# A macaron transformer layer on one core: the first quad's operands are spread by TensorE and its maxima added on chip, the opening runs in halves, and the steps of every batch are placed anew

## The chip, the cores and the metric

The kernel runs on one core of one Trainium2 chip. The metric is the device time of one execution in microseconds; the times given are medians of several runs. An engine has its own queue of instructions and runs it in order: TensorE (PE in the rows, PEld for its weight loads), VectorE (DVE), ScalarE (ACT), GpSimd (POOL) and SyncE (SP), which here issues most transfers. They wait for each other by semaphores alone.

## The reference

Eight batches of 512 tokens with 128 channels pass through half a feed-forward, attention, and half a feed-forward.

```python
x = x + 0.5 * ffn(layernorm(x), W1, b1, W2, b2)      # ternary W1, W2; ReLU; 128 -> 512 -> 128
x = x + attn(layernorm(x), Wq, bq, ...)              # 16 heads of 8 channels, RoPE on q and k
x = x + 0.5 * ffn(layernorm(x), W1, b1, W2, b2)
...
scores = einsum('bhnd,bhmd->bhnm', q, k) / sqrt(8)   # 512 x 512 per head and batch
attn = softmax(scores); out = einsum('bhnm,bhmd->bhnd', attn, v)
```

All of it is float32. The first feed-forward is called ffn1 here, the second ffn2.

## The kernel before

**Scores.** Heads go in pairs, eight pairs a batch, two pairs to a quad; the two heads of a pair lie in rows 0 to 63 and 64 to 127 of the array. q and k are each split into a high and a low part, and the four products of parts of eight channels fill 32 of a head's 64 rows. Rows 62 and 63 are for the maxima: k's hold -1 and q's the high and low part of each query's maximum, so that the second product comes out as score less maximum. The operands in that layout are `q_stack` and `k_stack`, with two slots for batches in turn. They are filled through memory: the parts go to `q_scratch` and `k_scratch` (`part_to_scratch`, L403), and from there as rows to the stack (`rows_to_stack`, L409). Rows that no transfer fills are set to zero by ScalarE (`zeros`, L796), and k's -1 by a transfer (`minus_between`).

**Steps.** A batch has 32 steps. In each, TensorE makes one score pair for the maxima (`m`, L541; VectorE reduces it, L906) and one transposed score pair (`e`, L560; ScalarE takes its exponential, L788). A burst `pv` (L577) multiplies four heads' probabilities with v. Score pairs lie in three units of PSUM in turn; one is free when its maximum or exponential has been taken. At the end of a quad VectorE splits the maxima, TensorE transposes them (`max_T`), ScalarE copies them and SP writes them into the stack.

**Order.** The lists FIRST (batch 0), STEADY (1 to 3) and LATER (4 to 7) give the order in words, the same for every engine: beside `e`, `m` and `pv` stand the side work of other batches (`ffn1_up0@3` is the first quarter of ffn1's hidden layer of batch 3), in one bank of PSUM, `side`. Each feed-forward is a transposition `T`, four `up` of two products (high and low part of x in float16) and four `down`. ffn1 runs four batches ahead, the projections two.

**Opening.** PROLOGUE lists what stands ahead of the steps: ffn1 of batch 0, T and up of batch 1, attention's transposition and first projections (`k_first`, `q_first`, each with a cosine and a sine part, rotated on VectorE, L983 to L989), v, down of batch 1 and T and up of batch 2. Then come eight maxima (OPEN_MAX), with down of batch 2 between the first four. Products with `ones_f` (`fill`, L652) write nothing that is used. The first quad's maxima go in as two half quads of four (`first_max_T`, L602, L760).

**End.** The last batch's attention output and ffn2 run in halves on all engines.

## Time and profile before

| | us |
|---|---|
| median of 3 runs | 520.1 (518.65 to 523.45) |
| the profiled execution, its time | 519.27 |
| its span | 517.5 |
| TensorE busy | 488.3 |
| VectorE busy | 409.2 |
| ScalarE busy | 347.5 |
| GpSimd busy | 203.5 |
| first score pair of TensorE at | 43.31 |
| its first transposed score pair at | 54.67 |
| last exponential ends at | 497.6 |

Busy time is a union of an engine's instructions; waits and issue are not in it. The ends of matmuls are modelled, so that a full TensorE is not at its peak. The granted clock is TensorE's, as a share of 2.4 GHz. A name after an arrow in brackets is what ended an engine's idle time.

### The profile page before, as it was taken

Reading aid. Unit: us, or ns where it says so; the run is one execution under the profiler, and the core shown is the slowest. Engines: PE = TensorE matmul, PEld = TensorE weight load, DVE = VectorE, ACT = ScalarE, POOL = GpSimd, SP = SyncE. Lnnn points to the kernel's source line nnn. Section 1 sums busy time; section 2 is a strip of 40 time slices with the busy share of each in tenths; the row PEclk is TensorE's granted clock in tenths of the full one; section 3 lists DMA queues with packets and bytes.
Section 4 is the critical chain, followed back from the end, with each engine's and each line's share of the span. In section 5 each row is a group of like instructions: output and inputs, shape, how many; then the busy total and the mean of one; then the engine's idle time right before and its main releaser. Section 6 shows DMA issues by size and latency. Waiting matters only on the chain.

```text
span 517.5 us, 13169 instructions
## 1 busy us (share of the span) xinstructions
PE 488.3 (94%) x5455; PEld 227.2 (44%) x5455; DVE 409.2 (79%) x644; ACT 347.5 (67%) x429; POOL 203.5 (39%) x226
## 2 busy tenths in 40 slices
PE   6689999899999999999999999999999999998996
PEld 3455435252354535363354533443344334443445
DVE  5776997958998689877897699779987998898124
ACT  5627565757767687577867677766776778578841
POOL 3507065707338080825534183336342650005001
PEclk8998999999999999999999999999999999999999
DMA  8047037203350136203450147024612451000000
GB/s 276 25 163 166 11 120 208 42 4 123 124 125 3 40 125 177 56 3 97 171 125 4 45 146 189 16 63 162 148 23 56 156 149 36 23 3 3 3 22 20
DMA packets 20007, 44.63 MB, mean 86 GB/s; under 512 B 2860, under 2 KB 5420, under 8 KB 18924
## 3 DMA queue, kind: packets, MB, share of 16 engines
q1 hardware_dynamic: 18636, 41.96, 28.4%
q10 hardware_dynamic: 1312, 1.84, 1.0%
q8 instruction: 43, 0.70, 0.6%
q14 instruction: 16, 0.13, 0.1%
HBM read 20.58 MB, written 18.87 MB: 76 GB/s over the span
## 4 chain that ended last, share of the span: by engine, by line
PE 72%; DVE 15%; ACT 6%; issue 3%; DMA 2%; POOL 1%; ACTq 0%; DVEq 0%; POOLq 0%
PE heads_acc L577 19%; PE side L584 18%; PE unit L560 14%; PE unit L541 12%; DVE maxima L906 8%; ACT probs L788 3%; ACT hidden L778 3%; PE side L621 2%; PE side L611 1%; DMA q_scratch<-q_parts 1%; PE heads_acc L652 1%; PE side L606 1%; PE unit L584 1%; DVE stats_ffn L873 1%; DMA resid<-in_x 1%
## 5 line engine op out<-in xcount | busy, mean ns | idle before, releaser
L906 DVE TENSOR_REDUCE maxima<-unit 128x2 f32<-128x1024 f32 x256 | 304.7, 1219 | 57.3 <-PE unit L541 56.4
L788 ACT ACTIVATE probs<-unit 128x1024 f32<-128x1024 f32 x256 | 256.2, 1025 | 99.1 <-PE unit L560 98.2
L577 PE MATMUL heads_acc<-probs,v_heads 128*32 128x512 f32 x1024 | 135.3, 601 | 0.6 <-ACT probs L788 0.4
L560 PE MATMUL unit<-q_stack,k_stack 64*128 64x512 f32 x512 | 118.7, 463 | 5.9 <-DVE maxima L906 5.3
L541 PE MATMUL unit<-k_stack,q_stack 62*128 62x512 f32 x512 | 114.0, 442 | 2.5 <-DVE maxima L906 1.0
L560 PEld LDWEIGHTS unit<-q_stack,k_stack 64*128 64x128 f32 x512 | 47.6, 184 | 72.6 <-DVE maxima L906 33.9
L541 PEld LDWEIGHTS unit<-k_stack,q_stack 62*128 62x128 f32 x512 | 48.3, 185 | 61.9 <-ACT probs L788 30.6
L584 PE MATMUL side<-w_q,hidden 128*32 128x128 f32 x1664 | 53.5, 275 | 0.0
L386 POOL TENSOR_TENSOR rope_a_k<-k,cos_t 128x512 f32<-128x512 f32 x7 | 8.9, 1277 | 101.6 <-ACT k L775 101.6
L584 PEld LDWEIGHTS side<-w_q,hidden 128*32 128x32 f32 x1664 | 43.2, 110 | 12.4 <-issue 8.9
L1062 POOL TENSOR_SCALAR var_eps_ffn<-mean_var_ffn 128x4 f32<-128x4 f32 x15 | 3.7, 249 | 108.1 <-DVE mean_var_ffn L877 108.1
L577 PEld LDWEIGHTS heads_acc<-probs,v_heads 128*32 128x32 f32 x1024 | 23.6, 108 | 36.9 <-issue 29.1
L778 ACT ACTIVATE hidden<-side,b_col 128x512 f32<-128x512 f32 x49 | 34.0, 693 | 8.0 <-PE side L584 7.7
L377 POOL TENSOR_SCALAR normed_ffn<-resid,mean_var_ffn,rstd_ffn 128x128 f32<-128x128 f32 x48 | 37.6, 795 | 1.3
L377 POOL TENSOR_SCALAR normed_attn<-resid,mean_var_attn,rstd_attn 128x128 f32<-128x128 f32 x28 | 21.9, 795 | 0.7
L584 PE MATMUL side<-x_hi,w_q 128*32 128x512 f16 x196 | 19.9, 393 | 1.5 <-ACT hidden L778 1.0
L652 PE MATMUL heads_acc<-ones_f 128*128 128x256 bf16 x124 | 18.9, 305 | 1.5 <-DVE ones_f L944 1.0
L584 PE MATMUL side<-x_lo,w_q 128*32 128x512 f16 x196 | 19.4, 384 | 0.0
L1075 POOL TENSOR_TENSOR xb_ffn<-resid,b_half 128x512 f32<-128x512 f32 x15 | 19.2, 1280 | 0.0
L941 DVE TENSOR_TENSOR resid<-side,xb_ffn 128x512 f32<-128x512 f32 x13 | 8.9, 687 | 12.0 <-PE side L584 12.0
L1062 POOL TENSOR_SCALAR var_eps_attn<-mean_var_attn 128x4 f32<-128x4 f32 x8 | 1.9, 231 | 39.8 <-DVE mean_var_attn L877 39.8
L1065 POOL TENSOR_TENSOR rstd_ffn<-var_eps_ffn,minus_half 128x4 f32<-128x4 f32 x15 | 15.6, 1043 | 1.4 <-POOL var_eps_ffn L1062 0.2
(144 smaller groups left out, 461.0 us busy)
## 6 DMA issues: line engine op xcount, KB each, us to landing
k_scratch<-k_parts SPq DMA_DIRECT2D x16, 512.0 KB, 2.9
q_scratch<-q_parts SPq DMA_DIRECT2D x14, 512.0 KB, 3.3
k_stack<-k_scratch SPq DMA_DIRECT2D x16, 384.0 KB, 5.4
q_stack<-q_scratch SPq DMA_DIRECT2D x16, 384.0 KB, 6.8
resid<-in_x SPq DMA_DIRECT2D x8, 256.0 KB, 4.8
k_stack<-k_scratch SPq DMA_DIRECT2D x16, 128.0 KB, 2.5
k_swap<-k SPq DMA_DIRECT2D x14, 128.0 KB, 2.3
q_swap<-q SPq DMA_DIRECT2D x14, 128.0 KB, 2.3
```

The source lines that it names most:

```text
L377: engine.tensor_scalar(normed[n][:, t, :], resid[:, j * T + t, :], mean_var[n][:, t, 0:1], rstd[n][:, t:t + 1], ALU.subtract, ALU.mult).th ...
L541: mm = pe.matmul(to[:, e, :], q_stack[part, quad // NQ % 2, pair, t * P:(t + 1) * P], k_stack[part, quad // NQ % 2, pair, :], start=True, ...
L560: mm = pe.matmul(to[:, e, :], k_stack[part, quad // NQ % 2, pair, kt * P:(kt + 1) * P], q_stack[part, quad // NQ % 2, pair, :], start=True ...
L577: mm = pe.matmul(heads_acc[32 * j:32 * j + 32, :], v_heads[:, b % 2, at, ODD * odd:ODD * odd + 32], probs[:, burst % RING, j, :], start=(k ...
L584: mm = pe.matmul(to[c:c + TILE_COLS, :], lhs[:, c:c + TILE_COLS], rhs, start=start, stop=stop)
L621: mm = pe.transpose(to[:, t * P:(t + 1) * P], normed[which][:, t, :], ident_f[:])
L652: pe.matmul(heads_acc[:, 0:2 * P], some[:, 0:P], some, start=True, stop=True)
L778: act.activation(hidden[:, arg, :], of, ACT.Relu, bias=b1_col[:, arg:arg + 1]).then_inc(s_hid[which], 1)
L788: act.activation(probs[:, burst % RING, 2 * pp:2 * pp + 2, :], unit_of(PLACE["exp", n]), ACT.Exp, scale=SCALE).then_inc(s_exp, 1)
L906: dve.tensor_reduce(maxima[:, quad % 2, :, r], unit_of(PLACE["max", k]), AX_X, ALU.max).then_inc(s_max, 1)
L1065: pool.tensor_tensor(rstd[n][:], var_eps[n][:], minus_half[:], ALU.pow).then_inc(s_rstd[n], 1)
L1075: pool.tensor_tensor(xb[n][:], batch_rows(j), bias.to_broadcast([P, T, D]), ALU.add).then_inc(s_xb[n], 1)
```

## The change

In the opening of batch 0 the operands of head pairs 0 and 1 no longer go through scratch. GpSimd makes 0/1 patterns (`spread`) out of the identity, and TensorE multiplies q's and k's parts with them, so that the 128 rows of the stack come out in PSUM (`spread_over`); ScalarE copies them into the stack, k's with -1 added in rows 62 and 63 (`minus_col`). For the first quad's maxima TensorE makes q's rows once more and adds the split maxima, transposed by a product with the identity, into the same bank (`rows_spread`, `rows_max`). The other pairs of batch 0 take the old way, all issued by SP.

Halves: ffn1's down of batch 0 lies in two banks, its residual is added in two halves, q's projection and rotation run in two halves of 256 columns. In the prologue products are 128 columns wide and not four times 32. GpSimd, and not VectorE, normalises batch 2 for ffn1. ScalarE's zeros come in pieces. At the end GpSimd's bias addition waits for the norm's last operation.

On TensorE's queue of the opening, from the last down quarter of ffn1 of batch 2 (L584) to the first transposed scores (L560; L541 are the maxima's scores), stood:

```order
L584 MATMUL side<-w_q,hidden 32x128 x16
L541 MATMUL unit<-k_stack,q_stack 128x512 x2
L652 MATMUL heads_acc<-ones_f 128x256 x4
L541 MATMUL unit<-k_stack,q_stack 128x512 x2
L652 MATMUL heads_acc<-ones_f 128x256 x4
L602 MATMUL heads_acc<-ident_f,first_parts 16x128
L541 MATMUL unit<-k_stack,q_stack 128x512 x4
L652 MATMUL heads_acc<-ones_f 128x256 x14
L560 MATMUL unit<-q_stack,k_stack 128x512 x2
```

The fillers (L652) and the four down quarters lay between and behind the eight maxima.

There, from the first spread on, stands now (L694 is the spread, L559 a maximum's scores, L602 side work):

```order
L694 MATMUL unit<-k_parts,spread 128x512 x2
L694 MATMUL heads_acc<-q_parts,spread 128x256 x2
L694 MATMUL unit<-k_parts,spread 128x512 x2
L559 MATMUL unit<-k_stack,q_stack 128x512 x2
L694 MATMUL side<-q_parts,spread 128x256 x2
L559 MATMUL unit<-k_stack,q_stack 128x512 x2
L694 MATMUL heads_acc<-q_parts,spread 128x512 x2
L559 MATMUL unit<-k_stack,q_stack 128x512 x2
L602 MATMUL side<-w_q,hidden 32x128 x16
```

Five spreads stand ahead of and between the first maxima, and down of batch 1 takes the place of batch 2's.

Where the opening ends and the steps begin, TensorE's queue now has (L709 is the transposed maxima, L578 transposed scores, L637 the transposition of batch 2's ffn1):

```order
L709 MATMUL heads_acc<-ident_r,max_cols 128x128 x4
L559 MATMUL unit<-k_stack,q_stack 128x512 x4
L578 MATMUL unit<-q_stack,k_stack 128x512 x2
L602 MATMUL side<-w_q,hidden 32x128 x16
L578 MATMUL unit<-q_stack,k_stack 128x512 x2
L602 MATMUL side<-w_q,hidden 32x128 x16
L559 MATMUL unit<-k_stack,q_stack 128x512 x2
L578 MATMUL unit<-q_stack,k_stack 128x512 x2
L637 MATMUL side<-ident_f,normed_ffn 128x128 x4
```

Half of batch 1's down and all of batch 2's ffn1, which were ahead of the first transposed scores, are behind them.

On VectorE's queue, from k's rotation to the first maxima, stood:

```order
L986 TENSOR_TENSOR rope_a_k<-rope_a_k,rope_b_k 128x512
L983 SCALAR_TENSOR_TENSOR rope_a_q<-unit,bqk_col,cos_t 128x512
L983 SCALAR_TENSOR_TENSOR rope_b_q<-unit,bqk_col,sin_t 128x512
L986 TENSOR_TENSOR rope_a_q<-rope_a_q,rope_b_q 128x512
L989 TENSOR_TENSOR k_parts<-rope_a_k,k_parts 128x512
L989 TENSOR_TENSOR q_parts<-rope_a_q,q_parts 128x512
L932 TENSOR_TENSOR v_heads<-unit,bv_rows 128x32x2x8
L377 TENSOR_SCALAR normed_ffn<-resid,mean_var_ffn,rstd_ffn 128x128 x4
L941 TENSOR_TENSOR resid<-unit,xb_ffn 128x512
```

Every operation covers all 512 columns, and the normalisation of batch 2 and what follows it stand ahead of the first maximum.

The same piece of VectorE's queue is now:

```order
L1077 TENSOR_TENSOR rope_a_k<-rope_a_k,rope_b_k 128x512
L1072 SCALAR_TENSOR_TENSOR rope_a_q<-unit,bqk_col,cos_t 128x256
L1072 SCALAR_TENSOR_TENSOR rope_b_q<-unit,bqk_col,sin_t 128x256
L1077 TENSOR_TENSOR rope_a_q<-rope_a_q,rope_b_q 128x256
L1081 TENSOR_TENSOR k_parts<-rope_a_k,k_parts 128x512
L1072 SCALAR_TENSOR_TENSOR rope_a_q<-unit,bqk_col,cos_t 128x256
L1081 TENSOR_TENSOR q_parts<-rope_a_q,q_parts 128x256
L1072 SCALAR_TENSOR_TENSOR rope_b_q<-unit,bqk_col,sin_t 128x256
L1077 TENSOR_TENSOR rope_a_q<-rope_a_q,rope_b_q 128x256
L1004 TENSOR_TENSOR v_heads<-side,bv_rows 128x32x2x8
L1081 TENSOR_TENSOR q_parts<-rope_a_q,q_parts 128x256
L978 TENSOR_REDUCE maxima<-unit 128x2 x4
```

q's rotation and split are in halves with k's split between them, and the normalisation, residual, x_lo and statistics that stood ahead of the first maximum are behind the maxima or on GpSimd.

The diff, cut:

```diff
-    "e m fill1", "e m first_max_T1", "e m m fill2 attn_T@1", "e m m fill2 k@1", "e m m q@1", "e m m ffn1_T@3",
...
+    "e ffn1_down2@1", "e ffn1_down3@1 m", "e attn_stats@1 ffn1_T@2", "e m first_rows1", "e m ffn1_up0@2",
+    "e m ffn1_up1@2 pv m", "e m ffn1_up2@2 pv attn_T@1",
...
-    "e m ffn1_T", "e m", "e pv m heads_copy1@-1 ffn1_up0", "e m pv max_T1", "e m", "e heads_T1@-1 pv m", "e m pv",
...
+    "e m ffn1_T", "e pv heads_copy1@-1 m", "e m ffn1_up0 pv", "e heads_T1@-1 m", "e m max_T1 pv ffn1_up1",
+    "e m out_T attn_stats", "e m", "e out pv m", "e m ffn1_up2 pv", "e m ffn1_up3", "e m pv max_T2", "e m ffn2_stats",
...
-    "e m ffn2_up3 pv attn_T", "e m", "e ffn2_down0 ffn2_down1 m", "e m ffn2_down2 ffn2_down3", "e m", "e pv max_T4 m",
-    "e m k pv q pv",
...
+    "e ffn2_down0 ffn2_down1 m", "e m ffn2_down2 ffn2_down3", "e m", "e pv attn_T m", "e m max_T4 pv", "e m k", "e m",
+    "e heads_T0 pv m", "e m q pv",
...
-            + [("attn_T", 0, 0, 0), ("k_first", 0, 0, 5), ("k_first", 1, 0, 6), ("q_first", 0, 0, 1), ("q_first", 1, 0, 2),
-               ("v", 0, 0, 3)]
-            + first_ffn("down", 1, [4]) + first_ffn("T", 2, [0]) + first_ffn("up", 2, [1, 2, 3, 0]))
+            + [("attn_T", 0, 0, 0), ("k_first", 0, 0, 5), ("k_first", 1, 0, 6)])
+HALF = S // 2
...
+SPREAD = [("k", 0, WHOLE, 5), ("q", 0, FIRST_HALF, HEADS_BANK), ("k", 1, WHOLE, 1), ("q", 0, SECOND_HALF, 0),
+          ("q", 1, WHOLE, HEADS_BANK)]
...
+MAX_NEEDS = [2, 2, 4, 4, 5, 5, 5, 5]
+OPENING_DOWN = ("ffn1_down", 0, 1, 0)
+OPENING = [("v", 0, 0, 0), ("fill", 4), ("spread", 0), ("spread", 1), ("spread", 2), ("max", 0), ("spread", 3), ("max", 1),
+           ("spread", 4), ("max", 2), ("ffn1_down", 0, 1, 0), ("max", 3), ("ffn1_down", 1, 1, 0), ("max", 4),
+           ("rows_spread", 0), ("max", 5), ("rows_max", 0), ("max", 6), ("max", 7)]
...
-FILL_BEFORE_MAX = 10
-FILL_BETWEEN_MAX = 4
-FILL_BEFORE_EXP = 14
-FILL_BESIDE_EXP = 4
...
-            for p in range(2):
-                sp.wait_ge(s_first_maxT, p + 1)
-                for e in range(2):
-                    sp.dma_start(q_stack[64 * e + ROWS_MAX:64 * e + ROWS_EXP, 0, p, :].bitcast(F32),
-                                 first_max_T[p][e * PARTS * T:(e + 1) * PARTS * T, :]).then_inc(s_first_maxrow[p], 16)
+            stack(0, slice(2, 4), s_stack_first[0])
+            stack(0, slice(4, NPAIR), s_stack[0])
...
+                for word in " ".join(PLANS[b]).split() if b < B else ():
+                    if word == "ffn2_down3" and b > 0:
+                        sp.wait_ge(s_y, b)
+                        sp.dma_start(out[b - 1].rearrange("(p t) d -> p t d", t=T), batch_rows(b - 1)).then_inc(s_stored, 16)
+                    elif word == "max_T4" and on("values", b):
+                        max_row((b + 1) * NQ)
+                    elif word in ("k", "q") and on("proj", b):
+                        swap(word, b + 2)
...
+            def spread_over(n, pair, cols, to, last):
+                for c in range(PARTS):
+                    mm = pe.matmul(to, spread[:, pair, "qk".index(n), c, :], qk_parts[n][:, c, cols], start=(c == 0),
+                                   stop=(last and c == PARTS - 1))
+                return mm
+
+            def rows_spread(pair):
+
+                if pair == 0:
+                    pe.wait_ge(s_first_stack, len(SPREAD))
+                else:
+                    pe.wait_ge(s_first_rows, pair)
+                spread_over("q", pair, WHOLE, heads_acc[:], False)
+
+            def rows_max(pair):
+                pe.wait_ge(s_first_split, (pair + 1) * SPLIT_STEPS)
+                for t in range(T):
+                    mm = pe.matmul(heads_acc[:, t * P:(t + 1) * P], max_cols[:, t, :], ident_r[:], start=False, stop=(t == T - 1))
+                mm.then_inc(s_first_rows_psum, 1)
+
+            pe.wait_ge(s_late, 16 * LATE_CONST_DMAS)
+            pe.wait_ge(s_spread, SPREAD_SET)
...
+            def take_spread(place):
+                n, pair, cols, b = SPREAD[place]
+                act.wait_ge(s_spread_psum, place + 1)
+                if n == "k":
+                    act.activation(spread_to(n, pair, cols), bank_of(b)[:, cols], ACT.Identity, bias=minus_col[:]).then_inc(s_first_stack, 1)
+                else:
+                    act.activation(spread_to(n, pair, cols), bank_of(b)[:, cols], ACT.Copy).then_inc(s_first_stack, 1)
+
+            def take_rows(pair):
+                act.wait_ge(s_first_rows_psum, pair + 1)
+                act.activation(spread_to("q", pair, WHOLE), heads_acc[:], ACT.Copy).then_inc(s_first_rows, 1)
...
+            zeros("k", 0, slice(2, NPAIR), True)
...
+                    zeros("q", 0, slice(2, NPAIR), True)
+                    zeros("k", 1, slice(0, 4), False)
+                if use[:3] == ("ffn1_up", 0, 1):
+                    zeros("k", 1, slice(4, NPAIR), True)
+                if use[0] != "k_first":
...
+            zeros("q", 1, slice(0, 4), False)
+            act.wait_ge(s_first_rope["k"], 3)
+            first_hi("k", WHOLE)
+            act.wait_ge(s_first_rope["q"], 3)
+            first_hi("q", FIRST_HALF)
+            act.wait_ge(s_minus, 3)
+            take_spread(0)
+            take_spread(1)
+            act.wait_ge(s_first_rope["q"], 6)
+            first_hi("q", SECOND_HALF)
+            take_spread(2)
+            take_spread(3)
+            take_spread(4)
+            zeros("q", 1, slice(4, NPAIR), True)
+            take_rows(0)
...
+            for h, ts in enumerate(ends):
+                dve.wait_ge(*((s_first_down, 1) if h == 0 else (s_down["ffn1"], 1)))
+                dve.wait_ge(s_xb["ffn1"], 1)
+                ready = s_first_x1 if h == 0 else s_x1
+                dve.tensor_tensor(resid[:, ts, :], tokens_of(5 + h)[:, ts, :], xb["ffn1"][:, ts, :], ALU.add).then_inc(ready, 1)
+                dve.wait_ge(ready, 1)
+                for t in range(ts.start, ts.stop):
+                    dve.bn_stats(stats["attn"][:, t, :], resid[:, t, :]).then_inc(s_stats["attn"], 1)
...
+            first_rope("k", 0, WHOLE, 5, 1)
+            first_rope("k", 1, WHOLE, 6, 2)
+            first_sum("k", WHOLE, 2)
+            first_rope("q", 0, FIRST_HALF, 1, 3)
+            first_rope("q", 1, FIRST_HALF, 2, 4)
+            first_sum("q", FIRST_HALF, 2)
+            first_lo("k", WHOLE, 1)
+            first_rope("q", 0, SECOND_HALF, 3, 5)
+            first_lo("q", FIRST_HALF, 1)
+            first_rope("q", 1, SECOND_HALF, 4, 6)
+            first_sum("q", SECOND_HALF, 5)
             dve.wait_ge(s_v_fill, 2)
             dve.wait_ge(s_bv, 1)
-            side_part(("v", 0, 0, 3))
-            ln_apply(dve, "ffn1", 2)
-            side_part(("ffn1_down", T - 1, 1, 4))
-            side_part(("ffn1_T", 0, 2, 0))
-            ln_stats("attn", 1)
-            ln_stats("ffn1", 3)
+            side_part(("v", 0, 0, 0))
+            first_lo("q", SECOND_HALF, 2)
...
+            for pair in range(2):
+                for n in "kq":
+                    for c in range(PARTS):
+                        pattern = spread[:, pair, "qk".index(n), c, :].rearrange("p (e r) -> p e r", e=2)[:, :, 0:PROD]
+                        pattern = pattern.rearrange("p e (q k d) -> p e q k d", q=PARTS, k=PARTS)
+                        to = pattern[:, :, c, :, :] if n == "q" else pattern[:, :, :, c, :]
+                        pool.tensor_scalar(to, channels[:, :, :, pair].unsqueeze(2).to_broadcast([P, 2, PARTS, DH]), 1.0, 0.0,
+                                           ALU.mult, ALU.add).then_inc(s_spread, 1)
+            pool.tensor_scalar(ident_r[:], ident_f[:], 1.0, 0.0, ALU.mult, ALU.add).then_inc(s_spread, 1)
...
+            pool.wait_ge(s_normed["attn"], T)
+            ln_apply(pool, "ffn1", 2)
+            pool.wait_ge(s_first_lo["q"], 2)
...
+            pool.wait_ge(s_end_normed, T)
```

## Rows read from the trace of the kernel before

**Rows 1.** The page's first part: each engine's busy us, share of the span, instructions.

```profile
PE 488.3 (94%) x5455; PEld 227.2 (44%) x5455; DVE 409.2 (79%) x644; ACT 347.5 (67%) x429; POOL 203.5 (39%) x226
```

**Rows 2.** Busy us per stretch: length, engines (instructions), granted clock, DMA share, GB/s.

```profile
54.64:121.90 67.26, 63.14 (x681) 26.98 (x681) 54.46 (x81) 42.34 (x54) 29.42 (x32) 1.00 0.28 77
...
121.90:180.80 58.90, 57.45 (x688) 26.41 (x684) 50.13 (x75) 41.75 (x53) 27.18 (x31) 1.00 0.30 85
...
239.20:296.50 57.30, 57.08 (x686) 26.44 (x688) 47.26 (x66) 41.49 (x52) 23.90 (x25) 1.00 0.31 90
296.50:348.30 51.80, 51.40 (x522) 21.76 (x524) 44.71 (x62) 38.05 (x47) 24.86 (x26) 1.00 0.37 103
```

**Rows 3.** The chain of waits, 26 to 56 us: start us, length us, what.

```profile
34.30 6.04 DMA q_scratch<-q_parts
...
40.72 2.45 DMA q_stack<-q_scratch
```

**Rows 4.** Timeline of the opening: start us, length us, engine, line, operation.

```profile
16.23 3.62 ACT L799 ACTIVATE q_stack<-ones_f 128x4096 fp32r<-128x4096 f32 x1
...
23.64 2.42 ACT L778 ACTIVATE hidden<-unit,b_col 128x512 f32<-128x512 f32 x4 [2.23 <-PE unit L584]
...
26.62 0.60 ACT L767 ACTIVATE x_T<-side 128x512 f32<-128x512 f32 x1 [0.56 <-PE side L621]
...
28.56 0.75 DVE L983 SCALAR_TENSOR_TENSOR rope_a_k<-unit,bqk_col,cos_t 128x512 f32<-128x512 f32 x1 [2.76 <-PE unit L628]
...
30.14 0.69 DVE L986 TENSOR_TENSOR rope_a_k<-rope_a_k,rope_b_k 128x512 f32<-128x512 f32 x1
...
49.48 0.26 DVE L882 TENSOR_SCALAR first_parts<-maxima 128x8 fp32r<-128x8 f32 x1
...
49.86 4.85 DVE L906 TENSOR_REDUCE maxima<-unit 128x2 f32<-128x1024 f32 x4
...
54.67 0.50 PE L560 MATMUL unit<-q_stack,k_stack 64*128 64x512 f32 x2 [0.54 <-issue]
```

**Rows 5.** Timeline, TensorE: transposes, hidden products, down, scores, fillers.

```profile
20.12 0.66 PE L621 MATMUL side<-ident_f,normed_ffn 128*128 128x128 f32 x4
...
22.98 0.40 PE L584 MATMUL unit<-x_hi,w_q 128*32 128x512 f16 x4 [2.20 <-DVE x_lo L927]
...
31.86 3.68 PE L584 MATMUL unit<-w_q,hidden 128*32 128x128 f32 x128
...
39.42 0.68 PE L584 MATMUL unit<-x_hi,w_q 128*32 128x512 f16 x4
...
43.31 0.51 PE L541 MATMUL unit<-k_stack,q_stack 62*128 62x512 f32 x2 [0.40 <-DMA q_stack<-q_scratch]
...
55.34 0.61 PE L652 MATMUL heads_acc<-ones_f 128*128 128x256 bf16 x4
```

**Rows 6.** Busy time per stretch around 39 us; columns as in the second group.

```profile
36.00:39.00 3.00, 1.46 (x17) 0.86 (x21) 2.12 (x9) 0.60 (x1) 0.00 (x0) 0.93 0.88 325
39.00:41.00 2.00, 2.00 (x24) 0.79 (x16) 1.35 (x12) 0.00 (x0) 1.50 (x3) 0.50 0.49 142
```

**Rows 7.** Timeline of the last batch's second half.

```profile
505.02 0.60 DVE L1039 TENSOR_SCALAR normed_ffn<-resid,mean_var_ffn,rstd_ffn 128x128 f32<-128x128 f32 x2 [0.23 <-POOL rstd_ffn L1135]
...
505.92 1.25 POOL L1138 TENSOR_TENSOR xb_ffn<-resid,b_half 128x512 f32<-128x512 f32 x1
505.97 1.54 DVE L1039 TENSOR_SCALAR normed_ffn<-resid,mean_var_ffn,rstd_ffn 128x128 f32<-128x128 f32 x2 [0.35 <-POOL rstd_ffn L1135]
...
508.46 0.42 DVE L1044 TENSOR_TENSOR x_lo<-side,x_hi 128x256 f16<-128x256 f32 x1 [0.61 <-ACT x_hi L857]
```

**Rows 8.** Timeline, rows of maxima of quad 1.

```profile
69.35 0.27 ACT L764 ACTIVATE max_T<-side 32x128 f32<-32x128 f32 x1 [1.09 <-PE side L606]
...
72.44 0.19 PEld L560 LDWEIGHTS unit<-q_stack,k_stack 64*128 64x128 f32 x2 [0.42 <-DMA q_stack<-max_T]
```

**Rows 9.** The page, a group: count, busy us, mean ns, idle us.

```profile
L377 POOL TENSOR_SCALAR normed_ffn<-resid,mean_var_ffn,rstd_ffn 128x128 f32<-128x128 f32 x48 | 37.6, 795 | 1.3
```

276 lines of the change are left out of this document (144 added, 132 removed), and 26 rows, old and new, of tables (FIRST, LATER, STEADY).

## The prediction

> **What bounds the kernel now.** I read the engine shares first [rows 1]: TensorE is busy for 488.3 of 517.5 us, VectorE for 79%, ScalarE for 67%. That says "TensorE", but as an average over stages. So the second view is the busy time per stretch, cut where TensorE starts the first exponential score of a batch [rows 2]. The reader is to see three things in it. Batches 1 and 3, with both feed-forwards, take 58.9 and 57.3 us and leave TensorE 1.5 and 0.2 us idle; the first batch takes 67.26 us and leaves it 4.1 us idle; batch 4, where ffn1 has run out, takes 51.8 us. From the second batch on the time is therefore the amount of TensorE work, and nothing that another engine is spared shows there.
>
> The opening is another matter. The chain of waits [rows 3] has two transfers in a row before the first score: 6.04 us until q's parts have landed in scratch, 2.45 us until they are back in the stack, with an issue between them. The timeline of the opening [rows 4] shows what surrounds it: x_T ready at 27.22, k rotated at 30.83, last part of q at 34.3 (the start of the transfer in rows 3), first score at 43.31 [rows 5], the eighth maximum at 54.71, and TensorE's first exponential score at 54.67. In that last stretch VectorE's maxima, 1.22 us each, run almost without a break, so they are what paces it.
>
> **Term 1: when the first exponential score starts.** I rebuild the opening's chain from rows.
>
> ScalarE is the late one before x_T. Zeroing eight pairs took 3.62 us [rows 4]; the change zeroes six pairs (2.7), then four (1.8), then after x_hi (0.6) another four (1.8). From 16.23: 18.9, 20.8, x_hi by 21.4, 23.2. Four ReLUs take 2.42 and the copy 0.60 [rows 4]. With a slip of 0.2 for the hidden products x_T is ready at 26.4, 0.8 earlier than 27.22. The residual in halves gains about 0.7 on VectorE and the layer norm without GpSimd's bias beside it up to 1.0, but both end under ScalarE's chain, so I cost them at nothing. Cover of the same kind hides the nine new GpSimd copies (eight patterns, one identity). Their price is not in the trace. The nearest row is GpSimd's normalisation of 128 elements a partition at 0.8 us [rows 9]; the eight patterns have 32. Bounds: nothing, or 0.8 each, 7 us on GpSimd ahead of its first bias addition. I take 0.35 for a pattern and 0.8 for the identity, 3.6 in all, which puts that bias (due on VectorE at 18.5) at about 20, within the cover. At the far end x_T would be about 3 us later.
>
> From x_T on VectorE is the chain. x_T to the first product taken was 1.34 us, and k's three operations took 2.27 [rows 4]: k is rotated at 30.0. Then come eight operations on half the columns at 0.41 (a 256-column operation of this kind in [rows 7]), k's second part and v at 0.69 each: 4.7 us, the first maximum at 34.65. The spread itself runs beside this. It is two products of 512 columns (a pair of scores took 0.51 [rows 5]) and a copy of 0.6 to 0.7 per operand, and each of the first three is in the stack before VectorE comes free. Two scores are held back by the fourth and fifth spread for about 0.5 us each, under a maximum of 1.22.
>
> The first exponential score needs the unit of the sixth maximum, and the rows of the first four. Four maxima 4.9, the split 0.4 [rows 4], two more maxima 2.4: 42.4. The rows (products 0.4, copy 0.7 after the split) are there at 41.2, earlier. TensorE's own work from 32 on (eight score pairs, five spreads, v, two quarters of ffn1's down, the rows) is about 10.5 us, so it just fits. **42.4 against 54.67 is 12.2 us earlier.** The filler products disappear inside this stretch and are not counted again.
>
> **Term 2: work that was ahead of that point and now stands behind it.** Half of ffn1's down of batch 1: half of 3.68 [rows 5], 1.8 us. The whole ffn1 of batch 2: a batch with ffn1 less its neighbour without (57.3 less 51.8) is 5.5, batch 1 less the same is 7.1 with over an us of idle in it [rows 2]; the transposes at 0.66 and down at 3.68 [rows 5] are 4.3 of it. I take 6.0. **Plus 7.8.**
>
> **Term 3:** the second pair's maxima go in by a spread of q (0.51) and four transposing products (0.66) in place of one transpose of 0.3. **Plus 0.9.** Behind them wait that pair's exponentials. **Term 4:** three groups of four fillers at 0.61 [rows 5] go out of the first batch. **Minus 1.8.**
>
> **Term 5: idle time closed.** The first batch has 4.1 us of idle TensorE and gets 6.9 us more work (7.8 and 0.9 less 1.8). VectorE's busy 54.46 us there grow by some 4 (statistics, x_lo and residuals that were ahead) and by 2.9 us of maxima still open at the first exponential. That is 61 against TensorE's 70. With TensorE more clearly the bound the idle time should come near that of batches 1 to 3. Bounds 0 and 3.9. **I take minus 2.7**, nearer the batches that are bound by TensorE throughout.
>
> **Term 6: the last batch's norm.** The second two norm operations took 1.54 us beside GpSimd's bias addition of 1.25, the first two 0.60 [rows 7]. The change lets the addition wait for them; the result is needed by the last residual, 7 us later. **Minus 0.9**, bounds 0 and 0.95.
>
> **Term 7: the steps placed anew in batches 1 to 7.** The amount of work is the same. Idle time there is 0.2 to 1.5 us a batch [rows 2], so at best some 3 us come back. At worst a step is placed too near the one that it needs. The trace has no such wait; the nearest is the 0.4 us at 72.44 [rows 8]. Half a dozen of it would be 2.4 us. I take 0. One more edit is of SP's queue: the output, the swaps and the fourth maxima now stand in the order in which they are produced, which gates nothing that I see. Head pairs 2 to 7 of batch 0 still go through scratch, now issued by SP alone.
>
> **Sum:** -12.2 + 7.8 + 0.9 - 1.8 - 2.7 - 0.9 = -8.9. The span of 517.5 becomes 508.6; its run took 519.27, 1.8 more, and so the forecast is **510.4 us**. That run is 0.8 under the median of 520.1, whose runs spread from 518.65 to 523.45. About 1% (5.2 us) is what I hold for distinguishable.
>
> **What the clock could do.** Between 36 and 39 us TensorE was busy for 1.46 of 3 us, and its granted clock then was 0.50, the 1.2 GHz level, from 39 to 41 [rows 6]. A group of hidden products took 0.68 us there and 0.40 at full clock [rows 5]. The change takes away the wait behind which this happened, and also every filler between the maxima. The Trainium skill ("TensorE: Matmul & The Clock Gate", section "HAM oscillation — how this bites in real kernels") says that waits between bursts of matmuls re-throttle the array; by that rule an opening without fillers would lose its clock, which is rival B, and the trace's fall at 39 us agrees with it. By the rows of batch 0 alone, where TensorE is full, the sum stands as it is.
>
> **Rivals.**
> *A, the handover at quad 1 is late.* q's last part is ready at 34.65; 6.04 for scratch, four issues at about 0.45, 2.45 to land [rows 3] give 44.95. TensorE comes to the first score of quad 1 at 42.4 + 2 x 0.43 + 2 x 0.92 = 45.1. There is no slack. For it: both transfers of q and k now share the queue of SP. Against: VectorE is at its eighth maximum until 45.3 and then has 1.25 us of statistics. From 1 us of lateness on, each us costs one. At 3 us: 512.5 to 513.
>
> *B, half clock in the opening.* The 10.5 us of TensorE work between 32 and 42.4 run at the low level for 2 to 4 us (it lasted at least from 39 to 41 [rows 6]) and take 1.7 times as long there [rows 5]. That is 1.4 to 2.8 us, little of it covered, since the stretch is full: up to 513. For it: no fillers. Against: by my count the engine is kept busy in it.
>
> *C, VectorE and TensorE take turns in the first batch.* Up to the sixteenth maximum VectorE has, from 45.3, eight maxima, the statistics, x_lo, a residual and the split: to about 58.2. TensorE has 16.9 us from 42.4: to 59.3. Where two engines are both full, each waits a little for the other. Then term 5 is 0 instead of -2.7 and 1.5 more is lost: 514.6.
>
> *D, slower: the rows of maxima come late in each batch.* From ScalarE's copy to the score that uses it 3.1 us passed [rows 8], and TensorE waited 0.4 for the transfer. In the steady plan the transpose for a batch's second quad stands one step (1.8 us) nearer the score that needs it, which leaves three steps, some 5.4 us. It decides once VectorE runs more than 2.3 us behind. To be slower than 525.3 it must cost 16.7 us more than the sum above over seven batches, 2.4 us in each. Against: the other three quads' transposes are not nearer, the fourth even three steps earlier. This ends at 526.
>
> *E, all idle time closed*, terms 5 and 7 at their good ends: 506 to 507.
>
> **Chances.** Forecast as worked out 0.56; A 0.12; B 0.08; C 0.13; D 0.05; E 0.06. Faster by over 1% means below 514.9: all but D, half of C and the far ends of A and B (0.02 and 0.015), so 0.85; within 1% 0.10; slower 0.05. The forecast's own range is 508 to 513. The range that holds eight in ten takes in E and most of A, B and C: 506 to 515.
>
> **What would show it.** The first exponential score at 42 to 43 us (term 1), x_T at 26.4, the first maximum at 34 to 35. TensorE's first exponential score of batch 1 at 121.9 - 12.2 + 4.2 = 113.9 (terms 2 to 5); if it is at 116 or later, C holds, and idle time between 42 and 60 says whether A does. Stretches of batches 1 to 7 as long as now, within 1 us each (term 7). The last norm pair at 0.6 us (term 6). The granted clock between 30 and 45 at 1.00. The prediction is wrong if the first exponential score is later than 45, or if any later batch grows by over 1 us.

## The result and the profile after

The change did not make the kernel faster; it made it 0.5% slower. The changed kernel takes **522.8 us** (median of 20 runs, 519.4 to 527.2) against 519.3 for the kernel before on the same chip; the ratio is 1.0052, with a 95% interval of 1.0034 to 1.0070. The forecast was 510.4 us, range 506 to 515. The profiled execution took 521.89 us, its span 520.1.

The page after, engine shares, against [rows 1]:

```profile
PE 486.5 (94%) x5295; PEld 229.5 (44%) x5295; DVE 417.6 (80%) x650; ACT 350.3 (67%) x437; POOL 208.7 (40%) x239
```

TensorE does 160 products less, VectorE is busy for 8.4 us more with six more instructions. Of those 8.4 us, 6.8 lie in 62 small operations that both kernels have, as shown below.

Busy time per stretch of the changed kernel, cut where ScalarE starts the first exponential of a batch, against [rows 2]: batches 0, 1, 3, 4 and 6.

```profile
41.70:121.10 79.40, 72.51 (x904) 33.95 (x903) 60.88 (x100) 46.22 (x59) 38.60 (x45) 0.98 0.28 76
121.10:178.70 57.60, 56.09 (x686) 26.43 (x684) 50.32 (x74) 41.53 (x53) 29.94 (x33) 1.00 0.31 88
...
235.80:292.90 57.10, 56.00 (x686) 26.63 (x686) 48.85 (x66) 41.49 (x52) 23.87 (x26) 1.00 0.31 90
292.90:349.40 56.50, 52.64 (x524) 22.14 (x520) 49.09 (x64) 38.41 (x48) 32.12 (x33) 0.97 0.33 91
...
403.00:456.00 53.00, 50.88 (x504) 21.73 (x500) 44.23 (x57) 36.80 (x44) 6.88 (x8) 0.97 0.30 87
```

Batch 4 took 51.8 us before and takes 56.5 now; VectorE is busy there for 49.09 us where it was 44.71 [rows 2]. Cut in this way in both kernels:

| us | first exponential | batch 0 | 1 | 2 | 3 | 4 | 5 | 6 | 7 | last exponential to end |
|---|---|---|---|---|---|---|---|---|---|---|
| before | 55.2 | 67.4 | 58.8 | 58.3 | 57.3 | 51.8 | 52.6 | 50.9 | 45.4 | 19.8 |
| after | 41.7 | 79.4 | 57.5 | 57.1 | 57.1 | 56.5 | 53.6 | 53.1 | 44.7 | 19.4 |
| difference | -13.5 | +12.0 | -1.3 | -1.2 | -0.2 | +4.7 | +1.0 | +2.2 | -0.7 | -0.4 |

The sum is +2.6, the difference of the spans. The opening gave what was forecast; batch 0 took nearly all of it back, and batches 4 to 6 lost 7.9 us on top.

The opening, timeline of the changed kernel (start us, length us):

```profile
14.36 1.79 POOL L1193 TENSOR_SCALAR spread<-ident_f 128x32 fp32r<-128x32 f32 x8
16.12 0.29 POOL L1195 TENSOR_SCALAR ident_r<-ident_f 128x128 fp32r<-128x128 f32 x1
...
24.84 0.62 ACT L821 ACTIVATE x_T<-side 128x512 f32<-128x512 f32 x1
...
28.38 0.69 DVE L1077 TENSOR_TENSOR rope_a_k<-rope_a_k,rope_b_k 128x512 f32<-128x512 f32 x1
...
33.53 4.80 DVE L978 TENSOR_REDUCE maxima<-unit 128x2 f32<-128x1024 f32 x4
...
41.16 0.49 PE L578 MATMUL unit<-q_stack,k_stack 64*128 64x512 f32 x2 [0.31 <-DVE maxima L978]
```

x_T is ready at 25.46 (26.4 forecast), k rotated at 29.07 (30.0), the first maximum at 33.53 (34.65), the first exponential score at 41.16 (42.4).

What costs the time in batch 4 is in its timeline, GpSimd and VectorE:

```profile
295.64 1.29 POOL L403 TENSOR_TENSOR rope_a_q<-q,cos_t 128x512 f32<-128x512 f32 x1
296.03 0.94 DVE L963 TENSOR_SCALAR max_parts<-maxima 128x16 fp32r<-128x16 f32 x1
...
296.88 1.27 POOL L1175 TENSOR_TENSOR xb_out<-resid,rows 128x512 f32<-128x512 f32 x1
297.00 1.19 DVE L965 TENSOR_TENSOR max_parts<-maxima,max_parts 128x16 fp32r<-128x16 f32 x1
...
298.11 2.35 DVE L978 TENSOR_REDUCE maxima<-unit 128x2 f32<-128x1024 f32 x2
...
298.34 0.27 PE L619 MATMUL side<-ident_f,max_parts 128*32 128x128 f32 x1 [1.35 <-DVE max_parts L965]
```

The two small operations that split a quad's maxima for the transposition have 16 elements a partition. Here they took 0.94 and 1.19 us. Each began while a GpSimd operation of 512 elements was running, and each ended when that one did (296.93 and 296.97; 298.15 and 298.19). TensorE, which transposes their result next in its queue, stood for 1.35 us. What they cost otherwise is in the view of the tile `max_parts` (number, then ns minimum, median, maximum):

```profile
L963 DVE TENSOR_SCALAR max_parts<-maxima x31: 174/175/1382, 58.8 to 483.8; 128x16 fp32r<-128x16 f32 x31
L965 DVE TENSOR_TENSOR max_parts<-maxima,max_parts x31: 174/176/1304, 59.0 to 484.0; 128x16 fp32r<-128x16 f32 x31
...
its engine sat idle before it (us, times) until:
...
  DVE max_parts L965: 4.8, 3
```

The median is 0.175 us. I call a split over 0.8 us *held*, and the sum of all 62 less 0.174 each their *excess*. Before, 5 were held and the excess was 7.6 us; after, 13 and 14.4 us. All 13 started while a GpSimd operation was running and ended 29 to 36 ns after one: ten of them after that same operation, three (1.38 us each) after the bias addition that GpSimd began 0.06 us into them. In all the traces of this case 76 splits start inside a GpSimd operation with two inputs of 512 elements, and none ends ahead of it. The kernel before had it too, in its batch 1:

```profile
126.76 1.28 POOL L1075 TENSOR_TENSOR xb_out<-resid,rows 128x512 f32<-128x512 f32 x1
126.86 1.21 DVE L893 TENSOR_TENSOR max_parts<-maxima,max_parts 128x16 fp32r<-128x16 f32 x1
```

The Trainium skill ("SBUF — State Buffer", section "Who interferes with whom") says that VectorE and GpSimd share a port pair as an exclusive lock, that an operation of VectorE with two inputs in SBUF meets it, and that the later one waits for the whole instruction of the other. The rows agree for the second split, whose two inputs are in SBUF. The first split, a `tensor_scalar` with one input, was held likewise; why it is, no run here shows. The maxima, which read PSUM, keep their 1.22 us beside GpSimd. "The whole instruction" does not fit GpSimd's normalisations (128x128, 0.79 us): in the kernel before, a split that began 0.17 us into one took 0.30 us, another 0.50 us into one took 0.18, and both ended ahead of it.

The granted clock of the changed kernel, per stretch, against [rows 6]:

```profile
36.00:39.00 3.00, 3.00 (x62) 1.84 (x54) 2.84 (x5) 1.61 (x1) 0.00 (x0) 1.00 0.41 143
...
80.00:82.00 2.00, 1.08 (x12) 0.37 (x4) 1.97 (x8) 1.48 (x2) 1.89 (x3) 0.98 0.02 6
82.00:85.00 3.00, 3.00 (x38) 1.90 (x38) 2.56 (x3) 0.12 (x1) 2.92 (x5) 0.50 0.80 238
300.00:304.00 4.00, 4.00 (x20) 1.37 (x20) 3.41 (x5) 2.03 (x2) 2.63 (x3) 0.57 0.42 154
```

The opening stayed at full clock. Instead the clock was at its 1.2 GHz level for 3.4 us at 81.9, 300.4 and 436.9 us, the first after a stretch with 1.08 us busy of 2.00, the second after the wait of 1.35, the third after waits of 0.68 and 0.40 us. Not every wait brings a fall: waits of 1.75 us at 339.5 and 1.74 us at 393.0 brought none. At half speed 3.4 us cost some 1.7.

### The profile page after: what moved, and what is told of

Its sections match the earlier page's. It is cut to its first block, busy times and chain, and to the rows that moved or that the text cites. A ratio compares the mean times of both kernels' runs of the same rounds, so it can differ in the third digit from the quotient of the medians.

```text
span 520.1 us, 12883 instructions
## 1 busy us (share of the span) xinstructions
PE 486.5 (94%) x5295; PEld 229.5 (44%) x5295; DVE 417.6 (80%) x650; ACT 350.3 (67%) x437; POOL 208.7 (40%) x239
## 4 chain that ended last, share of the span: by engine, by line
PE 73%; DVE 15%; ACT 7%; issue 3%; DMA 1%; POOL 1%; DVEq 0%; POOLq 0%; ACTq 0%
PE heads_acc L595 20%; PE side L602 19%; PE unit L578 14%; PE unit L559 12%; DVE maxima L978 9%; ACT hidden L832 3%; DVE max_parts L963 2%; ACT probs L842 2%; PE side L637 1%; PE side L624 1%; PE side L619 1%; PE side L629 1%; DMA resid<-in_x 1%; PE heads_acc L670 1%; ACT k_stack L854 1%
## 5 line engine op out<-in xcount | busy, mean ns | idle before, releaser
L978 DVE TENSOR_REDUCE maxima<-unit 128x2 f32<-128x1024 f32 x256 | 305.6, 1220 | 52.9 <-PE unit L559 51.8
L578 PE MATMUL unit<-q_stack,k_stack 64*128 64x512 f32 x512 | 118.3, 461 | 8.3 <-DVE maxima L978 6.6
L559 PE MATMUL unit<-k_stack,q_stack 62*128 62x512 f32 x512 | 114.6, 445 | 1.8 <-DVE maxima L978 0.9
L578 PEld LDWEIGHTS unit<-q_stack,k_stack 64*128 64x128 f32 x512 | 48.1, 185 | 81.6 <-DVE maxima L978 41.7
L559 PEld LDWEIGHTS unit<-k_stack,q_stack 62*128 62x128 f32 x512 | 48.6, 186 | 46.6 <-issue 21.2
L602 PE MATMUL side<-w_q,hidden 128*32 128x128 f32 x1792 | 56.1, 274 | 0.1
L602 PEld LDWEIGHTS side<-w_q,hidden 128*32 128x32 f32 x1792 | 47.4, 110 | 13.4 <-issue 11.7
L832 ACT ACTIVATE hidden<-side,b_col 128x512 f32<-128x512 f32 x52 | 35.7, 687 | 12.7 <-PE side L602 12.7
L394 POOL TENSOR_SCALAR normed_ffn<-resid,mean_var_ffn,rstd_ffn 128x128 f32<-128x128 f32 x52 | 40.7, 795 | 2.5 <-DVE normed_attn L394 1.3
L602 PE MATMUL side<-x_hi,w_q 128*32 128x512 f16 x208 | 20.7, 386 | 2.3 <-ACT hidden L832 0.9
L602 PE MATMUL side<-x_lo,w_q 128*32 128x512 f16 x208 | 20.4, 379 | 0.0
L602 PEld LDWEIGHTS side<-x_hi,w_q 128*32 128x32 f16 x208 | 5.6, 94 | 22.5 <-ACT hidden L832 8.8
L818 ACT ACTIVATE max_T<-side 32x128 f32<-32x128 f32 x31 | 8.0, 259 | 11.1 <-PE side L619 11.1
```

Of the source, the lines that this page charges most:

```text
L394: engine.tensor_scalar(normed[n][:, t, :], resid[:, j * T + t, :], mean_var[n][:, t, 0:1], rstd[n][:, t:t + 1], ALU.subtract, ALU.mult).th ...
L559: mm = pe.matmul(to[:, e, :], q_stack[part, quad // NQ % 2, pair, t * P:(t + 1) * P], k_stack[part, quad // NQ % 2, pair, :], start=True, ...
L578: mm = pe.matmul(to[:, e, :], k_stack[part, quad // NQ % 2, pair, kt * P:(kt + 1) * P], q_stack[part, quad // NQ % 2, pair, :], start=True ...
L602: mm = pe.matmul(to[c:c + width, :], lhs[:, c:c + width], rhs, start=start, stop=stop)
L832: act.activation(hidden[:, arg, :], of, ACT.Relu, bias=b1_col[:, arg:arg + 1]).then_inc(s_hid[which], 1)
L978: dve.tensor_reduce(maxima[:, quad % 2, :, r], unit_of(PLACE["max", k]), AX_X, ALU.max).then_inc(s_max, 1)
```

## The experiments

All ratios are to the kernel before on the same chip. *Lists* are STEADY and LATER, the order of the steps in batches 1 to 3 and 4 to 7.

**e1: the change with the old lists.** The new opening and first batch stay.

```diff
-    "e m ffn1_T", "e pv heads_copy1@-1 m", "e m ffn1_up0 pv", "e heads_T1@-1 m", "e m max_T1 pv ffn1_up1",
+    "e m ffn1_T", "e m", "e pv m heads_copy1@-1 ffn1_up0", "e m pv max_T1", "e m", "e heads_T1@-1 pv m", "e m pv",
...
```

> The changed kernel with the old lists STEADY and LATER; opening and FIRST as changed. Theory 'plans' (the new lists lose 7.9 us in batches 4 to 6 and win 3.3 us in 1 to 3): those batches go back to 58.9, 58.4, 57.3 and 51.8, 52.5, 50.9 us, in all about 4.5 us less than the changed kernel, ratio to the kernel before 0.997. Theory 'first batch' (all that is lost is lost in batch 0 and in what it hands on): no more than 1 us less than the changed kernel, ratio 1.004. Batch 0 stays at 80 us in both.

517.1 us, ratio 0.9937 [0.9902, 0.9971]; 7 splits held, excess 9.3 us. Batches 4 to 6 are back at 51.9, 52.4 and 51.0 us. So their loss comes with the lists, and even then opening, batch 0 and end together are worth 3 to 4 us, not 9. The trace is of a run of 521.6 us, 4.5 over the median: its clock fell at 83.2 and 130.9, and its batch 1 took 61.8 us where 58.9 was expected.

**e2: the kernel before with the new lists** (and SP's queue in their order).

```diff
-    "e m ffn1_T", "e m", "e pv m heads_copy1@-1 ffn1_up0", "e m pv max_T1", "e m", "e heads_T1@-1 pv m", "e m pv",
+    "e m ffn1_T", "e pv heads_copy1@-1 m", "e m ffn1_up0 pv", "e heads_T1@-1 m", "e m max_T1 pv ffn1_up1",
...
```

> The kernel before with the new lists STEADY and LATER and the order of SP's queue that follows them; its opening and FIRST. Theory 'plans': the losses of batches 4 to 6 come along, 3 to 5 us more than before, ratio 1.007. Theory 'first batch': within 1 us of the kernel before.

526.4 us, ratio 1.0097 [1.0067, 1.0127]; 12 held, excess 13.2 us (trace of a run of 528.4). The lists alone cost 5 us, without the new opening. The timeline in batch 5 shows the pattern of 296 us again:

```profile
337.61 1.28 POOL L401 TENSOR_TENSOR k_parts<-rope_a_k,k_parts 128x512 fp32r<-128x512 f32 x1
337.70 1.22 DVE L891 TENSOR_SCALAR max_parts<-maxima 128x16 fp32r<-128x16 f32 x1
...
338.84 1.27 POOL L386 TENSOR_TENSOR rope_a_q<-q,cos_t 128x512 f32<-128x512 f32 x1
338.95 1.19 DVE L893 TENSOR_TENSOR max_parts<-maxima,max_parts 128x16 fp32r<-128x16 f32 x1
...
340.29 0.27 PE L606 MATMUL side<-ident_f,max_parts 128*32 128x128 f32 x1 [1.75 <-DVE max_parts L893]
```

**e3 and e4: GpSimd's operations in pieces**, in the changed kernel and in the one before. Same work, same order; what took one instruction of 512 columns takes four of 128. The copies of q's and k's high parts (0.62 us) stay whole.

```diff
+        def in_pieces(engine, to, a, b, op):
+            for c in range(0, S, P):
+                done = engine.tensor_tensor(to[:, c:c + P], a[:, c:c + P], b[:, c:c + P], op)
+            return done
...
-            engine.tensor_tensor(rope_a[n][:], qk[n][:], cos_t[:], ALU.mult).then_inc(s_rope[n], 1)
+            in_pieces(engine, rope_a[n], qk[n], cos_t, ALU.mult).then_inc(s_rope[n], 1)
...
-                pool.tensor_tensor(xb[n][:], batch_rows(j), bias.to_broadcast([P, T, D]), ALU.add).then_inc(s_xb[n], 1)
+                for t in range(T):
+                    added = pool.tensor_tensor(xb[n][:, t:t + 1, :], batch_rows(j)[:, t:t + 1, :], bias, ALU.add)
+                added.then_inc(s_xb[n], 1)
```

> The changed kernel with each 512-column operation of GpSimd (bias additions, rotations, low parts) cut into four of 128 columns; nothing else moves. Theory 'shared port' (VectorE's two small splits of the maxima wait for a GpSimd operation of 1.28 us to end, up to 1.4 us where 0.18 is their own time; TensorE then stands still and its clock falls): the splits come down to at most 0.5 us, the waits of 1.35 to 1.75 us ahead of the transposed maxima go, and with them the half clock at 300; 4 to 6 us less than the changed kernel, ratio 0.996. Theory 'placement' (the steps are simply too near each other): the same time within 1 us, or a little more as GpSimd's work gets longer.

> The kernel before with the same cut. Theory 'shared port': its splits lose 7.6 us against their least time, few of it on TensorE's path, so 1 to 2 us less, ratio 0.997. Theory 'placement': 1.000.

e3: **508.8 us**, 508.5 to 509.5, ratio 0.9760 [0.9723, 0.9797]; no split held (longest 0.56 us), excess 3.2 us, no fall of the clock in the span. e4: 518.9 us, 0.9959 [0.9933, 0.9986], excess 4.7. GpSimd itself is busy for longer in e3 (243.2 us for 208.7), and the kernel is 14 us faster, more than twice the 4 to 6 us that I had expected. The same place in e3, timeline:

```profile
290.68 0.17 DVE L970 TENSOR_SCALAR max_parts<-maxima 128x16 fp32r<-128x16 f32 x1
290.89 0.35 DVE L972 TENSOR_TENSOR max_parts<-maxima,max_parts 128x16 fp32r<-128x16 f32 x1
...
291.59 0.28 PE L626 MATMUL side<-ident_f,max_parts 128*32 128x128 f32 x1
```

Batch by batch, e3 against after: 78.3, 55.9, 55.9, 55.9, 51.8, 51.8, 51.6, 44.6. Beside what after's trace holds in each batch:

| batch | 0 | 1 | 2 | 3 | 4 | 5 | 6 | 7 |
|---|---|---|---|---|---|---|---|---|
| held splits, over 0.174 each, us | 1.1 | 2.2 | 2.2 | 2.2 | 3.8 | 2.0 | 0 | 0 |
| half clock, 1.7 us a fall | 1.7 | | | | 1.7 | | 1.7 | |
| after less e3, us | 1.1 | 1.6 | 1.2 | 1.2 | 4.7 | 1.7 | 1.4 | 0.0 |

In batch 7, the only one where nothing was held and no clock fell, the time is the same. The two rows above do not add up to the third everywhere: only what TensorE waits for shows in the time.

**e5 and e6: the same pieces with one half of the change each**: e5 has the new opening and the old lists, e6 the old opening and first batch with the new lists.

```diff
-            engine.tensor_tensor(rope_b[n][:], qk_swap[n][:], sin_t[:], ALU.mult).then_inc(s_rope[n], 1)
+            in_pieces(engine, rope_b[n], qk_swap[n], sin_t, ALU.mult).then_inc(s_rope[n], 1)
...
```

> The changed kernel with the old STEADY and LATER and GpSimd's operations in pieces. If the new lists are worse in themselves, this is under the 508.8 us of the changed kernel in pieces; if they lost only to GpSimd's long operations, it is over it: by the stretches of the kernels before and changed in pieces (57.7, 57.5, 57.2, 52, 51.8, 50.1 against 55.9, 55.9, 55.9, 51.8, 51.8, 51.6) about 4.5 us over, 513.

> The kernel before with the new STEADY and LATER and pieces: the old opening and FIRST in the same surroundings as the changed kernel in pieces. The difference of the two is what opening and FIRST are worth together. By their stretches (first exponential at 55.3, batch 0 67.5 us, against 41.6 and 78.4) 3 us more than 508.8: 512. The prediction's terms 1 to 5 would have it 8 us more: 517.

e5: 516.1 us, 0.9922 [0.9892, 0.9952]. e6: 514.5 us, 0.9895 [0.9863, 0.9926]. All eight together:

| ratio to before | GpSimd whole | in pieces |
|---|---|---|
| old opening, old lists | 1 | 0.9959 (e4) |
| old opening, new lists | 1.0097 (e2) | 0.9895 (e6) |
| new opening, old lists | 0.9937 (e1) | 0.9922 (e5) |
| new opening, new lists | 1.0052 (after) | 0.9760 (e3) |

With GpSimd's operations in pieces, the kernel gains 5.7 us from the rest of the change (e6 less e3) and 7.3 from the lists (e5 less e3), where I had expected 3 and 4.5; with them whole the lists cost 5 to 6. Neither gain is the worth of one thing. Of e6's, the traces have 12.8 us less ahead of the first exponential and 11.0 more in batch 0, so 1.8 for the opening; 1.3 are in batch 6 and 2.6 at the end, where e6 keeps the old end and its clock fell at 426.8 and 501.9. Of e5's, 5.1 us are in batches 1 to 3 and 3.2 in batch 4, and those 3.2 the pieces brought: batch 4 of the old lists takes 51.8 and 51.9 us with GpSimd whole (before, e1) and 55.1 and 55.0 in pieces (e4, e5). GpSimd ends a normalisation, which TensorE transposes, 20.6 us into the batch in e5, for 18.0 before; TensorE waits for it, and the clock falls at 315.3. In e5, timeline:

```profile
310.47 3.14 POOL L394 TENSOR_SCALAR normed_ffn<-resid,mean_var_ffn,rstd_ffn 128x128 f32<-128x128 f32 x4
...
313.76 0.63 PE L644 MATMUL side<-ident_f,normed_ffn 128*128 128x128 f32 x4 [2.09 <-POOL normed_ffn L394]
```

Against the old lists in their better form of each batch, GpSimd whole or in pieces, e3's batches 1 to 7 are some 3 us shorter; against the kernel before, 7.4.

**e7: padding.** The operations stay whole; two operations on one element stand ahead of each. This separates length from where an operation falls.

```diff
+        def padding(engine):
+            for k in range(2):
+                engine.tensor_scalar(pad[:, (j := next(pads)):j + 1], minus_half[:, 0:1], 1.0, None, ALU.mult)
...
+            padding(engine)
             engine.tensor_tensor(rope_a[n][:], qk[n][:], cos_t[:], ALU.mult).then_inc(s_rope[n], 1)
```

> A control for the pieces: the changed kernel with GpSimd's 512-column operations whole, and two one-element operations (about 0.23 us each) ahead of each, so that GpSimd's work is as long as in pieces while each long operation stays 1.28 us. Theory 'shared port': no gain, 520 to 526 us, splits of the maxima up to 1.4 us. Theory 'timing' (the pieces helped because GpSimd's work came later): near 509.

**511.2 us**, ratio 0.9825 [0.9782, 0.9867]. My expectation of 520 us and more failed. The trace has one held split, excess 3.1 us: the operations are as long as they were, but each starts 0.4 us later, and the splits now pass ahead of them or between them. Length sets the price of a collision; whether there is one is a matter of tenths of a us.

**e8: less TensorE work in the first batch.** e3 with most products of ffn1 of batch 2 left out, all hand-overs kept (its values are not computed).

```diff
-                        mm = column_tiles(width, to, w1_q[:, arg * P:(arg + 1) * P], part[:], n == 0, n == 1)
+                        mm = column_tiles(width, to, w1_q[:, arg * P:(arg + 1) * P], part[:], n == 0, thin or n == 1, thin)
...
-                    for n in range(FT):
+                    for n in range(1 if thin else FT):
```

> The changed kernel in pieces, with most of TensorE's work of ffn1 of batch 2 left out: one product of 32 columns in place of eight per hidden quarter and of sixteen per down quarter, all hand-overs kept. This takes about 4.9 us of array time out of batch 0. Theory 'work' (batch 0 is as long as TensorE's work there): batch 0 falls by 4.5 to 5 us from 78.3. Theory 'hand-overs' (one bank of PSUM, taken by ScalarE or VectorE between each two side steps, sets the pace): it falls by less than 2.5.

510.3 us, ratio 0.9811 [0.9776, 0.9847], no faster than e3. The timeline says why:

```profile
78.38 1.29 POOL L426 TENSOR_TENSOR q_parts<-rope_a_q,q_parts 128x128 fp32r<-128x128 f32 x3
...
79.70 0.36 SPq L433 DMA_DIRECT2D q_scratch<-q_parts  x1
80.10 1.41 SPq L501 DMA_DIRECT2D q_stack<-max_T  x2
...
82.89 0.80 PE L585 MATMUL unit<-q_stack,k_stack 64*128 64x512 f32 x2 [2.50 <-DMA q_stack<-max_T]
```

SP issues the third quad's rows of maxima behind q's transfer to scratch, which waits for GpSimd's last part of q. TensorE came earlier and waited for them, 2.50 us, and its clock then fell at 82.4. In e3 the same wait is 0.98 us.

**e9: the waits filled.** The change with four products of ones ahead of each transposition of maxima.

```diff
+                    for _ in range(ALIVE):
+                        pe.matmul(to[:, 0:2 * P], some[:, 0:P], some, start=True, stop=True)
                     pe.wait_ge(s_split, index * SPLIT_STEPS)
```

> The changed kernel, GpSimd whole, with four filler products (0.15 us each) into the side bank ahead of each transposition of the maxima, where TensorE waits for VectorE's split. It tells the clock's share from the waits' share. Theory 'clock' (most of the 13 us between whole and pieces is half clock after those waits): the falls of the granted clock at 82, 300 and 437 go, about 1.6 us each; 31 x 0.45 us of filler where there was no wait, 10 us or so, are against it, so 524 to 530 us with a granted clock of 1.00 from 20 us on. Theory 'waits alone': the falls stay.

528.1 us, ratio 1.0139 [1.0099, 1.0179]. The falls at 81.9 and 300.4 are gone, one is left in the steps (441.8). Splits are held as before (12, excess 13.3 us), and TensorE is busy for 495.2 us instead of 486.5. That fits a clock that falls behind waits; keeping it up in this way costs more than it gives back.

**e10 and e11: SP's order.** e3 and e8 with the third quad's rows of maxima issued ahead of q's transfer.

```diff
-                if on("values", b):
-                    to_scratch("q", b + 1)
                 if b == 0:
                     max_row(2)
+                if on("values", b):
+                    to_scratch("q", b + 1)
```

> The changed kernel in pieces, and in batch 0 SP writes the third quad's maxima ahead of q's parts of batch 1 and not behind them. Theory 'queue' (the seventeenth exponential score waits about 1 us for rows whose transfer stands behind GpSimd's q): the wait at 82.5 goes, 0.7 to 1.2 us less than 508.8, ratio 0.974. Rival: q's operands for batch 1 come later by the same and it is given back at batch 1's first maxima: no change.

> As the thin one (most of TensorE's work of ffn1 of batch 2 left out, all hand-overs kept), with SP's queue as in the run beside it. Theory 'queue': the thin kernel gained nothing since its seventeenth exponential waited 2.5 us in SP's queue; now the time left out shows, 2.5 to 4 us less than the kernel beside it with all its work. Theory 'hand-overs': still less than 1.5 us.

e10: 509.0 us, 0.9782 [0.9751, 0.9813], no different from e3: the wait of 0.98 is gone and batch 0 is 1.1 us shorter (77.3), but its profile has a fall of the clock at 423.4 that e3's has not. e11: 506.2 us, 0.9730 [0.9693, 0.9767]. Now the left-out work shows, 2.8 us. In e8 the queue had hidden it. By my estimate 4.9 us of TensorE's work were left out, so some 2 us of it still do not show, and the hand-overs are not excluded for them.

**e12: halves.** As e3, in two instructions of 256 columns.

```diff
-            for c in range(0, S, P):
-                done = engine.tensor_tensor(to[:, c:c + P], a[:, c:c + P], b[:, c:c + P], op)
+            for c in range(0, S, 2 * P):
+                done = engine.tensor_tensor(to[:, c:c + 2 * P], a[:, c:c + 2 * P], b[:, c:c + 2 * P], op)
```

> The changed kernel with GpSimd's 512-column operations in two instructions of 256 columns, between whole operations (522.8 us, its 62 splits of maxima 14.7 us over their shortest) and four pieces (508.8 us, 3.6 us over). Theory 'a split that starts inside a GpSimd operation is held to its end': no split can be held for more than about 0.65 us, so none takes over 0.85 us; the excess falls to 4 to 8 us and the time to 510 to 514 us. Rival 'it is where the instructions happen to fall, not how long they are': halves are a new phase like any other, and the time may lie anywhere from 509 to 523 us, with no bound on the longest split from their length.

511.9 us, ratio 0.9817 [0.9787, 0.9847]. Eleven splits took 0.65 to 0.85 us, none more, excess 6.8. One of them:

```profile
180.31 1.43 POOL L1183 TENSOR_TENSOR xb_out<-resid,rows 128x256 f32<-128x256 f32 x2
180.42 0.66 DVE L972 TENSOR_TENSOR max_parts<-maxima,max_parts 128x16 fp32r<-128x16 f32 x1
```

It started beside the first of the two halves (0.7 each) and was held by that one alone. The length of GpSimd's instruction bounds the split.

**e13: the padding of e7 in e2's kernel; e14: one element operation in place of two** in the changed kernel.

```diff
-            for k in range(2):
+            for k in range(1):
```

> Before's opening and first batch with the new lists (without padding 526.4 us, 12 splits over 0.8 us, 13.2 us over the shortest) and two one-element GpSimd operations ahead of each 512-column one, which leaves every operation whole and shifts where it starts. Theory 'the new lists' cost is a collision at fixed places': most of the 12 long splits miss their GpSimd operation, at most 3 are left, and the time is 513 to 518 us, near the 514.5 us that the pieces gave. Rival 'the new lists are slower in themselves, and padding helped only the new opening': 522 to 527 us.

> The changed kernel with one one-element GpSimd operation ahead of each 512-column one in place of two: half the shift. Theory 'phase': the time follows the splits' excess over their shortest whatever it comes to, by the line through the two kernels measured (14.7 us over at 522.8, 3.4 us over at 511.2: about 1 us of time for each us). So a run with 3 to 5 us over is at 510 to 513, one with 12 to 15 at 520 to 523. Rival 'the gaps between operations let VectorE in, whatever the phase': half the padding gives about half the gain, 516 to 518 us, with the long splits each cut short rather than fewer.

e13: 515.7 us, 0.9888 [0.9858, 0.9918]; 3 held, excess 5.2. So the padding cures the new lists with the old opening too, 10.7 us under e2. e14: **509.8 us**, 0.9773 [0.9749, 0.9797]; 3 held, excess 3.3. Half of the padding gives all of the gain, and the few splits that are still held (0.85, 0.85, 1.19 us) last to the end of GpSimd's whole operation, 28 to 31 ns after it, as before. That speaks against "gaps let VectorE in" and for the phase. At the place of 296 us, e14's VectorE:

```profile
291.31 0.21 DVE L973 TENSOR_SCALAR max_parts<-maxima 128x16 fp32r<-128x16 f32 x1
291.56 0.17 DVE L975 TENSOR_TENSOR max_parts<-maxima,max_parts 128x16 fp32r<-128x16 f32 x1
```

and its GpSimd, whose operation of 512 comes 0.07 us behind the second split's start:

```profile
291.46 0.21 POOL L401 TENSOR_SCALAR pad<-minus_half 128x1 f32<-128x1 f32 x1
291.63 1.28 POOL L410 TENSOR_TENSOR rope_a_q<-q,cos_t 128x512 f32<-128x512 f32 x1
```

With new opening and new lists, the kernel with the large excess is the slow one: 14.4 us at 522.8 (after), 6.8 at 511.9 (e12), 3.1 at 511.2 (e7), 3.3 at 509.8 (e14), 3.2 at 508.8 (e3). Among the last four it does not order the times. All four beat both kernels.

## Why the prediction was wrong

Two steps failed. The larger error, 7.8 us, is batch 0, and 5.5 of it is term 5: idle time that was to shrink by 2.7 us grew by 2.8. The other, 4.5 us, is term 7, put at nothing. With batch 0 right the forecast would still have been 3.7 us short, with term 7 right 7.0.

**Term 1 was right** and a little cautious: -13.5 us for -12.2. GpSimd's nine patterns took 2.1 us, not the 3.6 assumed, and ScalarE's chain gave x_T 0.9 earlier than forecast; from x_T ready to the first exponential score, 15.7 us passed where I had 16.0. Rival A did not come: between 42 and 60 us TensorE was idle for 1.0 us in all, none of it behind a transfer. Rival B did not come: the clock was 1.00 from 30 to 44 us, and without fillers TensorE was busy for 3.00 of the 3 us from 36 to 39, so the waits that B's rule needs were not there.

**Terms 2 to 4** were mis-sized. Each TensorE step of batch 0 priced at the median of its kind over these kernels gives 61 to 62 us before and 69 to 71 after, an estimate of some 8.5 us for my 6.9. The batch as a whole grew by 12.0 us where the sum had 4.2.

**Term 5 failed in sign.** It closed 2.7 us of idle time; the rows have TensorE idle for 4.1 us of batch 0 before (67.26 less 63.14 [rows 2]) and for 6.9 after (79.40 less 72.51), so it opened 2.8. Rival C had this as turns between VectorE and TensorE, and it named the test: batch 1's first exponential score at 116 or later. It came at 120.5. C's mechanism is not what most of the idle time shows, though: after, TensorE's waits for the maxima are 1.1 us of it, before 2.0. What the runs show is one held split at 75.85 us and the clock at half at 81.9 (e3, without both: 1.1 us shorter), the queue of SP (0.98 us in e3, gone in e10, 1.1 us), and hand-overs of TensorE's one side bank, in e3 and e10 alike at 59 (0.81), 74 (0.86) and 93 us (0.75). The last I read from the traces and did not take away in a run. The first two are 2.2 of the 7.8 us; how the rest divides between hand-overs and mis-sized work stays open.

**Term 7 failed too**, and it is why the change lost and did not win a little. I had "the amount of work is the same" and bounded it by -3 and +2.4. Both bounds were wrong, and in opposite directions:

- Where nothing is held, the new lists gain: 5.1 us in batches 1 to 3 (e5 less e3), 3 to 7 in all. I had taken TensorE's idle time, 0.2 to 1.5 us a batch, as all that could come back. But TensorE's busy time can shrink too. The same stretch, batch 2, of e5 and then of e3:

```profile
177.70:235.70 58.00, 56.92 (x686) 26.38 (x684) 48.20 (x74) 41.51 (x52) 33.05 (x64) 1.00 0.31 89
```

```profile
175.80:231.70 55.90, 55.78 (x686) 26.56 (x684) 48.53 (x74) 41.40 (x53) 33.09 (x65) 1.00 0.33 92
```

The same 686 products at the same clock are busy for 1.14 us less. In batch 3 of the kernel before 57.08 of 57.30 us looked full [rows 2]; e3 does it in 55.9. From the start of eight value products to a transposition behind them 1.17 us passed on average in batch 2 of before (up to 1.79), 1.00 in e3. I read this as a matmul's recorded end running on into a wait behind it; that a change of step costs the time itself is not excluded.

- The new lists put steps on VectorE and GpSimd so that more splits of the maxima start shortly after a GpSimd operation has begun. Together with the one in batch 0, which the old lists have as well, that costs 12 to 14 us: 522.8 to 508.8 with four pieces, to 511.2 and 509.8 with the start shifted and the length kept. No rival named it. D had the right victim, the rows of maxima, and the wrong cause: not their distance in steps, but the 0.175 us operation ahead of them. "Gates nothing that I see" held for the outputs; SP's order at the third quad, which the change left as it was and which cost nothing before, cost 1 us in batch 0. D's price was also off: 16.7 us is 525.3 less the span of 508.6, and less the forecast of 510.4 it is 14.9, 2.1 us a batch.

**Term 6 was half right.** Timeline of the last batch, against [rows 7]:

```profile
508.61 0.60 DVE L1139 TENSOR_SCALAR normed_ffn<-resid,mean_var_ffn,rstd_ffn 128x128 f32<-128x128 f32 x2 [0.23 <-POOL rstd_ffn L1252]
...
509.56 0.60 DVE L1139 TENSOR_SCALAR normed_ffn<-resid,mean_var_ffn,rstd_ffn 128x128 f32<-128x128 f32 x2 [0.35 <-POOL rstd_ffn L1252]
...
510.33 1.26 POOL L1256 TENSOR_TENSOR xb_ffn<-resid,b_half 128x512 f32<-128x512 f32 x1 [0.81 <-DVE normed_ffn L1139]
```

The second pair takes 0.60 us as forecast, for 1.54, and the end comes 0.4 us sooner, not 0.9. It is the same effect as in batch 4: a normalisation held by GpSimd's addition. I read it in [rows 7], priced it for one place, and did not ask where else VectorE has small operations on a chain that TensorE waits for.

The sum of the errors against the table above: -1.3 (term 1), +7.8 (batch 0), +4.5 (batches 1 to 7), +0.5 (end) is the 11.5 us between the spans of 508.6 and 520.1. e3's 508.8 us would have met the forecast, but by luck: its batch 0 is 6.8 us over the sum and its batches 1 to 7 are 7.4 under.

## What to carry to other kernels

Where VectorE and GpSimd work side by side, look at the minimum, median and maximum of the smallest operations that a chain waits for: a maximum of 1.2 us over a median of 0.175 is a collision, and every new order of steps moves where they fall. Cut the other engine's operations into pieces, or shift them, before judging an order of steps, or the order's own worth stays hidden (here some 3 to 7 us of gain looked like 5 to 6 us of loss); then look whether the longer work now makes another engine wait, as it did in batch 4 of e4 and e5. And a TensorE that looks busy for over 99% of a stretch (batch 3 before) can still give 1.4 us of 57 back.

## What the runs showed of the hardware

- A VectorE operation of 16 elements a partition that starts inside a two-input GpSimd operation of 512 (at 0.73 us or sooner) ends some 30 ns after it, however short it is: 0.175 us alone, 1.30 us when it starts 0.01 us into it (after, 75.85), 0.94 at 0.38 us, 0.58 at 0.73 us. Halves of 0.7 us hold it for 0.65 us in most cases; among quarters of 0.47 us the longest split took 0.56.
- A one-element operation on GpSimd takes 0.22 us, and one ahead of each large operation was enough to lose 10 of 13 collisions (e14).
- Four GpSimd pieces of 128 columns take 1.72 us where the whole takes 1.28 (`rope_a_q` in e3 and in after); the kernel with the dearer form is the faster one.
- Waits of TensorE of 0.9 to 2.5 us were followed by 3.4 us at the 1.2 GHz level: 81.9 and 300.4 in after, 82.4 in e8, 341.7 and 396.3 in e2 (waits of 1.76 and 1.77). The waits of 1.75 and 1.74 us at 339.5 and 393.0 in after were not. The fall near 425 to 440 us in after, e7, e10 and e12 has no wait over 0.7 us ahead of it. What decides is open.
